# All values through DRAM by pairs of heads, maxima tile by tile, and the first heads' loads in the prologue: one change to a cross-attention and feed-forward kernel

## The reference

```python
q = (layernorm(x) @ Wq + bq), per head, times 1/sqrt(32)
k, v = split(ctx @ Wkv + bkv), per head
q = fq_sym(q, axis=-1)      # rounded to 127 steps of the row's largest |value|
k = fq_sym(k, axis=-1)
v = fq_sym(v, axis=2)       # the largest |value| over ALL 6404 keys, one for each column
attn = fq_unsigned(softmax(q @ k.T), axis=-1)
x = x + (attn @ v) @ Wp + bp
x = x + ffn(layernorm(x))   # block-quantised 512 -> 2048 -> 512
```

## Time and profile before

| | us |
|---|---|
| median of 3 runs | 2722.95 (2720.22 to 2727.97) |
| the profiled execution | 2737.58 |
| its span | 2735.8 |
| busy: TensorE, VectorE, ScalarE, GpSimd | 2249, 2493, 1983, 1420 |

### The profile page before, as it was taken

How to read it: one execution, slowest core, us unless ns; L and a number is a source line. 1 busy time by engine, 2 the same in 40 slices (tenths; PEclk the granted TensorE clock), 3 DMA queues, 4 the chain that set the end, 5 groups by cost and what they waited for, 6 DMA issues and landing times. The chain is left out here.

```text
span 2735.8 us, 52956 instructions
## 1 busy us (share of the span) xinstructions
PE 2249.1 (82%) x20003; PEld 1193.3 (44%) x20020; DVE 2492.6 (91%) x3592; ACT 1983.4 (72%) x1813; POOL 1419.5 (52%) x1855
## 2 busy tenths in 40 slices
PE   8899899968888888788888788888887777867886
PEld 4444454424444444444444444444444444433443
DVE  6998667879999999999999999999999999957997
ACT  3344333458888888888888888888988888864665
POOL 2432222136556575666757667675775758552001
PEclk9999999967677777777777876787777888779999
DMA  7565445489999999999999999999999999991000
GB/s 228 123 146 114 89 97 120 90 190 175 197 177 202 203 181 197 181 197 185 191 210 180 193 200 193 192 183 211 178 197 194 189 195 175 180 213 43 16 16 27
DMA packets 1389368, 442.13 MB, mean 162 GB/s; under 512 B 1323924, under 2 KB 1364372, under 8 KB 1387576
## 3 DMA queue, kind: packets, MB, share of 16 engines
q1 hardware_dynamic: 1378472, 397.08, 76.7%
q10 hardware_dynamic: 10736, 43.11, 6.3%
HBM read 78.99 MB, written 42.35 MB: 44 GB/s over the span
## 5 line engine op out<-in xcount | busy, mean ns | idle before, releaser
L888 DVE TENSOR_SCALAR_CACHE_REDUCE arena<-a_ps_s 128x1281 f32<-128x1281 f32 (+1 forms) x1280 | 1826.3, 1488 | 46.1 <-PE a_ps_s L833 38.1
L940 ACT ACTIVATE arena<-arena,a_bias,a_row_scale 128x3328 uint8<-128x3328 f32 (+1 forms) x512 | 1560.4, 3048 | 257.4 <-POOL a_bias L1003 255.7
L833 PE MATMUL a_ps_s<-arena,a_q_rep 96*128 96x512 bf16 (+2 forms) x3840 | 1232.4, 443 | 325.0 <-DVE arena L888 290.7
L846 PEld LDWEIGHTS a_ps_o<-a_v_head,a_nT 128*128 128x128 f16 x13056 | 529.6, 103 | 295.2 <-issue 160.9
L833 PEld LDWEIGHTS a_ps_s<-arena,a_q_rep 96*128 (+1 forms) x3840 | 314.6, 109 | 767.8 <-DVE arena L888 417.8
L1010 POOL CAST a_nT<-arena 128x1664 int16<-128x1664 uint8 x256 | 401.8, 1570 | 352.3 <-DMA arena<-arena 349.5
L846 PE MATMUL a_ps_o<-a_v_head,a_nT 128*128 128x32 f16 x13056 | 518.8, 183 | 43.4 <-POOL a_nT L1011 39.8
L1011 POOL CAST a_nT<-arena 128x1664 int16<-128x1664 uint8 x256 | 402.9, 1574 | 0.0
L358 POOL TENSOR_TENSOR p_rest<-p_kq,p_parts 128x512 f32<-128x512 f32 (+1 forms) x51 | 88.8, 1742 | 317.2 <-ACT p_parts L468 317.2
L999 POOL TENSOR_SCALAR a_row_max<-a_row_max,a_part_max 128x1 f32<-128x1 f32 x256 | 92.2, 360 | 246.6 <-DVE arena L888 229.3
L388 PE MATMUL p_ps_k<-p_wkv,p_ctxT 128*128 128x512 f32 (+1 forms) x408 | 190.3, 611 | 0.0
(11 more groups left out here) (151 smaller groups left out, 1943.0 us busy)
## 6 DMA issues: line engine op xcount, KB each, us to landing
k_parts_transposed<-p_stage SPq DMA_DIRECT2D x25, 768.0 KB, 7.0
p_ctx<-in_ctx_dram SPq DMA_DIRECT2D x25, 512.0 KB, 5.8
arena<-k_parts_transposed ACTq DMA_DIRECT2D x48, 240.1 KB, 4.0
late_values<-arena SPq DMA_DIRECT2D x51, 192.0 KB, 6.9
a_late_v<-late_values ACTq DMA_DIRECT2D x6, 1632.0 KB, 9.6
arena<-in_L_ffn_W_dram SPq DMA_DIRECT2D x8, 1024.0 KB, 8.1
arena<-k_parts_transposed ACTq DMA_DIRECT2D x48, 160.1 KB, 3.8
a_q_rep<-q_transposed ACTq DMA_DIRECT2D x48, 128.0 KB, 5.4
```

The source lines that it names most:

```text
L833: last = nc.tensor.matmul(ps_s[:, b, n0:n0 + w], q, k_parts[0:3 * HD, slot, start[c] + n0:start[c] + n0 + w], start=True, stop=True)
L846: last = nc.tensor.matmul(ps_o[:, u, 0:HD], nT[:, u, j, :], v_head[:, v_slot, j, :], start=(j == 0), stop=(j == KT - 1))
L888: nc.vector.tensor_scalar(s_row[:, u, start[c]:start[c] + size[c]], ps_s[:, (u + c) % 2, 0:size[c]], 1.0, None, ALU.mult, ALU.max, accum_o ...
L940: nc.scalar.activation(out, s_row[:, u, keys_of_half[half]], ACT.Exp, scale=row_scale[:, u, 0:1], bias=bias[:, u:u + 1], accum_out=zsum[:, ...
```

## The change

- Values no longer stay in the arena. A tile's values go into one of three places (`v_tile`), and all 512 columns (256 KB a tile) are stored to DRAM as numbers, by pairs of heads. VectorE's addition of tile t waits for the store of tile t-3 and for its absolute values.
- The largest values: ScalarE writes |v| of each tile (`vabs`) between its two copies of the keys' parts, and VectorE takes one maximum a tile, that of tile t-1 behind the addition of tile t.
- Only heads 0 and 1 are rounded in the prologue, from DRAM (`v_first`, one load of 1.67 MB behind all stores), and stay in SBUF (`v_head`). Heads 2 and 3 are rounded by GpSimd in the attention, like all others.
- The keys and queries of heads 0 and 1 are loaded by SyncE in the prologue: the keys and the first half of head 0's queries ahead of the stores of query tiles 8 to 15, the other queries behind them.
- In the attention one rounding operation stands in each of rows 3 to 14, ahead of the unpacking, and the scaling of a finished head moves from row 6 to row 15. Rows 4 to 15 of heads 0 and 1 are written out for TensorE.
- The last step of the bias parts works on one row instead of 96.

```diff
@@ constants, prepare(): the arena @@
-EARLY_HEADS = 4
 GROUP = 2
+EARLY_HEADS = GROUP
...
-    v32 = arena.rearrange("p (t c) -> p t c", c=C)
+    k_parts, q_rep, v_head, head_loaded, late_q_loaded = first
...
+    v_tile = view(3 * C).rearrange("p (u c) -> p u c", c=C)
+    stage = view(2 * 3 * CC * P).bitcast(BF16).rearrange("p (u n k) -> p u n k", u=2, k=2 * P)
+    vabs = view(2 * C).rearrange("p (u c) -> p u c", c=C)
+    v8 = view(GROUP * KT * HD // 4, I8).rearrange("p (h t d) -> p h t d", h=GROUP, d=HD)
...
+    v_first = arena[:, K:K + KT * GROUP * HD].rearrange("p (t c) -> p t c", c=GROUP * HD)
@@ prepare(), SyncE @@
-            def store_late_values(t):
+            def store_values(t):
                 sp.wait_ge(v_taken, t + 1)
-                sp.dma_start(late_v_dram[:, :, place(t), :].rearrange("g p c -> p g c"),
-                             v32[:, place(t), EARLY_HEADS * HD:C].rearrange(
-                                 "p (g c) -> p g c", c=GROUP * HD)).then_inc(late_v_stored, 16)
+                sp.dma_start(v_dram[:, :, place(t), :].rearrange("g p c -> p g c"),
+                             v_tile[:, t % 3, :].rearrange("p (g c) -> p g c", c=GROUP * HD)).then_inc(v_stored[t % 3], 16)
...
             for t in range(2 * PAIRS - 2, KT):
-                store_late_values(t)
+                store_values(t)
+            for i in range(3):
+                sp.wait_ge(v_stored[i], 16 * ((KT + 2 - i) // 3))
+            sp.wait_ge(b_stored, 16)
+            sp.wait_ge(w_bytes, PIECES)
+            sp.dma_start(v_first.rearrange("p t c -> p (t c)"),
+                         v_dram[0].rearrange("p t c -> p (t c)")).then_inc(v_first_loaded, 16)
+
+            sp.wait_ge(k_stored[0], 16 * ((PAIRS + 2) // 2))
+            sp.wait_ge(k_stored[1], 16 * ((PAIRS + 1) // 2))
+            load_keys(0)
+            for i in range(2):
+                sp.wait_ge(q_stored[i], 16 * (HALF_Q // 2))
+            load_queries(0, 0, head_loaded[0])
+            load_keys(1)
             for t in range(HALF_Q, QT):
-                if t > HALF_Q:
-                    store_query(t - 1)
-                for h in heads_beside(t):
-                    sp.wait_ge(v16_ready, h + 1)
-                    sp.dma_start(v_dram[h], v16[:, h % 2].rearrange("p t d -> p (t d)")).then_inc(v_stored[h % 2], 16)
-            store_query(QT - 1)
+                store_query(t)
             for i in range(2):
                 sp.wait_ge(q_stored[i], 16 * (QT // 2))
...
+            load_queries(0, 1, late_q_loaded[0])
+            for half in range(2):
+                load_queries(1, half, head_loaded[1] if half == 0 else late_q_loaded[1])
@@ prepare(), ScalarE @@
                 nc.scalar.activation(parts[0:r, 0, :], kq[0:r, :], ACT.Copy).then_inc(hi_ready, 1)
+                act.wait_ge(v_taken, t + 1)
+                after_first(act, vmax_done, t - 1)
+                nc.scalar.activation(vabs[0:r, t % 2, :], v_tile[0:r, t % 3, :], ACT.Abs).then_inc(vabs_ready, 1)
                 act.wait_ge(rest_ready, t + 1)
@@ prepare(), VectorE @@
-                if t == BIAS_TILE:
-                    dve.wait_ge(b_stored, 16)
-                if t == W_TILE:
-                    dve.wait_ge(w_turned, 2 * PIECES)
+                if t >= 3:
+                    dve.wait_ge(v_stored[t % 3], 16 * (t // 3))
+                    dve.wait_ge(vabs_ready, t - 2)
...
+            def largest_value(t):
+                r = rows(t)
+                dve.wait_ge(vabs_ready, t + 1)
+                after_first(dve, vmax_done, t)
+                nc.vector.tensor_tensor(v_scale[0:r, :], v_scale[0:r, :], vabs[0:r, t % 2, :],
+                                        ALU.max).then_inc(vmax_done, 1)
...
             def value_bytes(h):
-                after_first(dve, v16_ready, h - 1)
-                nc.vector.tensor_tensor(v8[:, h % 2], of_head(h), inverse_of(h, KT), ALU.mult).then_inc(v8_ready, 1)
+                if h == 0:
+                    dve.wait_ge(v_first_loaded, 16)
+                nc.vector.tensor_tensor(v8[:, h], of_head(h), inverse_of(h, KT), ALU.mult).then_inc(v8_ready, 1)
...
-                largest_values(t)
+                if t >= 1:
+                    largest_value(t - 1)
+                if t == FULL:
+                    largest_value(t)
@@ attention() @@
-    SUMS_AT, INVERT_AT, SCALE_AT = 2, 5, 6
-    ROUND_AT, ROUND_PARTS, RELOAD_AT = 7, 6, 14
+    SUMS_AT, INVERT_AT, SCALE_AT = 2, 7, 15
+    ROUND_AT, ROUND_PARTS, RELOAD_AT = 3, 6, 15
...
-                pe.wait_ge(head_loaded[slot], loaded * 144)
+                pe.wait_ge(head_loaded[slot], FIRST_LOADS if h < 2 else FIRST_LOADS + (loaded - 1) * 144)
...
+                if h < 2:
+
+                    for t in range(4, QT):
+                        if t == QT // 2:
+                            pe.wait_ge(late_q_loaded[h], 48)
+                        row_of_scores(h * QT + t, t, t % 2, slot, slot)
+                    return
...
-                after_first(act, v_rounded, group * GROUP * ROUND_PARTS)
-                act.dma_start(late_v[:], late_v_dram[group]).then_inc(
-                    late_v_loaded, 16)
+                after_first(act, v_rounded, (group - 1) * GROUP * ROUND_PARTS)
+                act.dma_start(late_v[:].rearrange("p t c -> p (t c)"),
+                              v_dram[group].rearrange("p t c -> p (t c)")).then_inc(late_v_loaded, 16)
...
             for row in range(ROWS):
-                maximum_and_unpack(row, row % 2)
-                head, part = row // QT + 1, row % QT - ROUND_AT
-                if EARLY_HEADS <= head < H and 0 <= part < ROUND_PARTS:
-                    round_values(head, part)
+                maximum(row, row % 2)
+                head, step = row // QT + 1, row % QT - ROUND_AT
+                if EARLY_HEADS <= head < H and 0 <= step < 2 * ROUND_PARTS:
+                    round_values(head, step)
+                if row >= 1:
+                    unpack(row - 1, 1 - row % 2)
```

154 lines of the change are left out of this document (62 added, 92 removed).

## The result

The changed kernel takes 2756.8 us (median; 2750.65 to 2762.58), the kernel before, run beside it, 2724.8: a ratio of 1.0118, 95% interval 1.0087 to 1.015. The forecast was 2761.5, slower. Medians and ratios are of the fast executions; one of experiment 6, which took 3153.5 us at a granted clock of 0.54, is left out. The profiled execution of after took 2752.27 us (span 2750.5), that of before 2737.58: 14.7 more, where the medians differ by 32. So I first ask where in the span the two profiles part.

The account below looks back on a forecast made before the run. VectorE was taken to bound the attention, while no engine is full in the prologue (TensorE nearest). Prologue +37, tail +1.5 and attention 0 sum to 38.5, so median 2722.95 becomes 2761.5 us; 8-in-10 range 2722 to 2792.

Parts of the forecast that it names:

- tile 3: Prologue, value addition of tile 3: first store at 43.1 plus 8.2 gives 51.3 against 43.8, +7.5 us.
- T3-21: Prologue, additions of tiles 3 to 21: nine pairs paced by the wait for value stores, 198 us against 167.3, +30.5.
- T21-37: Prologue stretch with queries, TensorE's 20.9 us a pair as floor: 173.8 us against 188.1, -14.3, from the lost bursts.
- T37-49: Prologue, additions of tiles 37 to 49: pairs of 17.6 to 20.7 us, 114.3 against 97.9, +16.5.
- tile 49: Prologue, value addition of tile 49: expected near 537 us.
- TensorE's lead, tail: Prologue's end: TensorE some 3 us ahead when keys end, -3; tail +11 for late stores and issues, -9.5 gap, net +1.5.
- attention: Attention, bound by VectorE: at most 27.3 us of waits to win, taken as 0; written-out rows 0 to 10 us.
- the landing: Prologue, issue to landing of a value store: 7.7 us early, 6.5 late, plus 0.5 for size: 8.2 and 7.0.
- The port: Prologue: two-input maximum blocks GpSimd's subtraction on the shared port, 0.6 us added to the loop, bounds 0 and 2.
- The maxima: Prologue, VectorE: 51 maxima replace 13 bursty reductions; VectorE gives back about 25 us, and above all the bursts.
- Rival 4: Tail: loads are there but the barrier moves back as much as the start gains; if they hide, 2752. No chance given.
- Rival 1: Prologue: stores land in time (4.6 us), additions do not wait, change is faster, 2705; chance 0.11.

Follow-up runs that it names:

- experiment 6: Changed kernel with the attention's GpSimd order of the kernel before (rounding in rows 7 to 12, behind the unpacking): 2751.2 us, ratio 1.0111.
- experiment 1: Changed kernel with four places for value tiles instead of three, nothing else: 2706.9 us, ratio 0.9934 to the kernel before.
- experiment 2: Changed kernel, three places, SyncE issuing the two value stores ahead of the pair's key store: 2708.3 us, ratio 0.9943 to the kernel before.
- Experiment 7: Changed kernel, three places, storing 96 KB of a tile's values instead of 256 KB: 2754.7 us, ratio 1.011 to the kernel before.
- two other profiles: Same prologue up to the last query stores: changed kernel with first loads behind those stores (2752.8 us), and with the old GpSimd attention order (2751.2 us).
- experiment 9: Changed kernel, three places, each maximum replaced by a one-input reduction of the same 128x512 values: 2743.0 us, ratio 1.0074 to the kernel before.
- experiment 3: Kernel before with only the maxima changed (Abs on ScalarE, one maximum per tile), no ring, no early loads: 2704.9 us, ratio 0.9926.
- experiment 5: Changed kernel with four places and the first heads' loads one by one between the query stores: 2703.3 us, ratio 0.9919 to the kernel before.

## Why the prediction was right, point by point

| step | forecast | measured |
|---|---|---|
| tile 3 | +7.5 | +4.2 |
| T3-21 | 198, +30.5 | 190.3, +23.0 |
| T21-37 | 173.8, -14.3 | 175.5, -12.7 |
| T37-49 | 114.3, +16.5 | 109.1, +11.3 |
| tile 49 | near 537, +40 | 522.9, +25.9 |
| TensorE's lead, tail | -3, +1.5 | +0.3 together |
| attention | 0 | -11.7 in one profile, 0 within the scatter |

- *The sign and its cause.* The addition waits for the store at odd tiles outside the query stretch, 3.5 to 7.8 us (forecast 3 to 6), 74.8 us in all ("over 60"), and experiments 1 and 2 take the loss away by two ways out of the same wait. Tile 3 was a little better than reckoned: its store left at 40.76 and not at 43.1, and landed after 7.2 us and not 8.2. Two of the 16 odd tiles, 7 and 11, did not wait. The pairs took 20.1 to 22.8 us up to tile 21 (forecast 20 to 22) and 16.8 to 19.9 after tile 37 (17 to 20).
- *The mis-sized term is the landing.* The legs were forecast as 8.85 us (tile 13 to 15: 1.4, 3.1, 3.4 and 0.95), 5.8 and 8.2, and the rows show 8.6, 5.7 and 6.5; the mean of the last is 7.5 early and 6.6 late, where I had 8.2 and 7.0, and 6.6 to 6.7 and 6.4 to 6.5 in the two other profiles of this prologue. I took the 7.7 us of one store and added 0.5 for its size. Experiment 7 shows nothing for the size, and the one store was on the long side: before, the median was 6.9. (The 13.0 us of that row is the landing of a load of values, as in the earlier trace rows; the stores alone took 4.6 to 7.8.) With 6.65 us in place of 8.2 the forecast's own sum for tiles 3 to 21 gives 184, and 184.2 and 184.9 were measured in the other two profiles.
- *The port.* 0.6 us was taken, within 0 and 2, and taking the second input away (experiment 9) gives 0.6 to 0.7 a pair: the size was about right. But the prediction priced GpSimd's side only. VectorE's two weight steps with two inputs took 2281 ns each before; in the changed kernel they take 3245 and 2885, and in the rows of tiles 13 to 15 above the step starts while GpSimd's subtraction runs. VectorE's groups up to 580 us, before and then after (busy, mean ns of one):

```profile
L618 DVE SCALAR_TENSOR_TENSOR arena<-arena,p_inverse 128x2048 int8<-128x2048 f32 x8 | 18.2, 2281 | 0.0
L624 DVE SCALAR_TENSOR_TENSOR arena<-arena,p_power 128x2048 bf16<-128x2048 int8 x8 | 18.3, 2281 | 0.0
```

```profile
L630 DVE SCALAR_TENSOR_TENSOR arena<-arena,p_inverse 128x2048 int8<-128x2048 f32 x8 | 26.0, 3245 | 0.0
L636 DVE SCALAR_TENSOR_TENSOR arena<-arena,p_power 128x2048 bf16<-128x2048 int8 x8 | 23.1, 2885 | 0.0
```

  That is 12.6 us of VectorE's time which the prediction did not count. The Trainium skill (SBUF — State Buffer, SBUF: two separate sides) says that whichever of the two engines starts first holds the shared pair for its whole instruction and the other blocks; both sides show here, GpSimd's subtraction with 1.60 against 1.15 us beside the maximum and VectorE's step with 3.24 against 2.28 behind that subtraction.
- *The query stretch: right in size, wrong in part of its cause.* I had some pairs bound by the ring there, and the first rival had 167.2 with the ring open. With no wait for a store it still takes 174.4 (experiment 1) and 174.2 (experiment 3). So the ring isn't what holds it. In experiment 1 tiles 22 and 23 show what may (VectorE, ScalarE, TensorE):

```profile
225.86 3.25 DVE L636 SCALAR_TENSOR_TENSOR arena<-arena,p_power 128x2048 bf16<-128x2048 int8 x1
...
229.14 1.26 DVE L661 TENSOR_SCALAR p_x<-p_x,p_mv,p_rstd 128x512 f32<-128x512 f32 x1
...
233.70 0.63 ACT L481 ACTIVATE p_parts<-p_kq 128x512 bf16<-128x512 f32 x1 [5.11 <-DVE p_kq L594]
...
238.99 0.84 PE L431 MATMUL p_ps_t<-ident,p_parts 128*128 128x128 bf16 x12 [1.95 <-ACT arena L513]
```

  The weight step, itself 1 us longer by the port, and the normalisations (L661) make VectorE's split late, with it ScalarE's copies, and TensorE waits 1.95 us for them. No run takes these steps away, so that they hold the whole stretch is read from this one pair and not shown.
- *The maxima.* "Above all the bursts" holds: experiment 3 has 13.9 us less in T21-37, 9.4 less in T3-21 and 25.2 less at tile 49. The maxima and their combining cost VectorE 19.9 us less (35.4 against 55.3), but the weight steps cost 14.5 more by the port, and its busy time up to v_column fell by 7.6 us only, from 420.3 to 412.7, where the prediction had about 25. What counted was that the work no longer comes in lumps. But the lumps were not all: of the 46 us that the prediction called stalls and laid to them, 26 are gone in experiment 3, and the rest stayed.
- *The tail.* The copy of query tile 10 waited for its store (5.97 us), v_column came 6.3 us later against tile 49 (forecast 7), the barrier 10.0 (11), and the gap fell from 10.73 to 1.05, 9.7 (9.5). (Before, v_column's copy stood at 551.13 and the first instruction behind the barrier at 553.73.) Rival 4's better case, in which the loads hide, was priced at -9.5; spread out (experiment 5) the tail is 63.8 us from tile 49 to the first score, 3.8 under before's 67.6 and 7.3 under the 71.1 of experiment 1.
- *Two errors met.* The prologue was forecast 12 us too long at the first score (38.5 against 26.2), and yet the median came within 4.7 of the forecast. The medians differ by 32.0, 5.8 more than the first scores of the two profiles. Where these 5.8 us lie can't be told from one profile of each: the attention alone varies by 18, and the prologue with three places by 7.6. By the two other profiles of that prologue the error at tile 49 is larger, 18 and 22 us where this one has 14. So the sign and the wait were forecast from the rows, but that the median came within 5 us of the forecast is partly luck.
- *Rival 1* (open ring, 2705) was the right picture of the kernel next to this one: at a landing of 4.9 and a store that goes early it is 2708.3 (experiment 2). It was wrong about this one because the shortest landing, 4.6 us, is not that of a store right behind 768 KB of keys: it belongs to the last three tiles, and those right behind the keys took 5.9 or more. Its sum also has a slip: late in the prologue it takes 3.6 us off pairs that were reckoned with 7.0, where 2.4 is meant, so 101 us and not 97 for tiles 37 to 49, and some 2709. The Trainium skill's fit (DMA: Bandwidth & Descriptors, Anatomy of one DMA), made for a copy of another queue kind, gives 2.6 us by estimate for 256 KB. The shortest landing of experiment 2 is 2.6, and no store in the changed kernel comes near, where the least is 4.8 (4.0 and 4.1 in the two other profiles).

## What to carry to other kernels

A ring is as long as the whole way from one use of a place to its next, and most of that way need not be the transfer: here 5.5 us of some 20 for a pair lay between ScalarE's copy and the store's issue, in a queue that waited for another store's data, and changing the order of two issues was worth as much as a fourth place. When a change gives up a place per item for a ring, add up that way from rows and compare it with the pace of the items before counting anything that the change saves. A load moved forward saves only what it doesn't push back: put it between the stores of the same queue, not ahead of them, and look at the barrier for what its issues cost.

## What the runs showed of the hardware that I had not expected

- Landings differ between profiles of the same code: the same 256 KB stores behind the same 768 KB have a median of 6.6, 6.1 and 6.1 us in three profiles, and in a ring that waits for them this moves tile 49 by up to 7.6 us. Why is open. The store's own size does not show: with 96 KB the median was 6.1, with 192 KB and no ring 6.0 (experiment 3), with 256 KB and four places 6.0 (experiment 1).
- Beside a two-input weight step the second subtraction takes 2.42 us instead of 1.16, and the step itself loses too: L636 took 3.25 us in the rows of experiment 1 above and 2.29 at 174.28 us after. The conflict costs both sides, not only the one that waits. A maximum moved by 0.7 us out of GpSimd's way was worth 6 us of prologue even with no ring to wait for.
- The attention, bound by VectorE, took between 1849 and 1868 us from one profiled execution to another with the same work; below some 10 us a single pair of profiles says nothing there, while the prologue repeats to 1 us as long as nothing waits for a store (tile 49 at 471.9, 471.9, 471.1 and 471.4 in four kernels with no ring or four places).
